# Second attention rebuilt: maxima four pairs ahead, queries turned again by four heads, output rows token-major, last-layer tiles inside

## The reference

```
x = x + attn0(cond(x)); x = x + ffn0(cond2(x))
x = x + attn1(cond3(x)); x = x + ffn1(cond4(x))
```

## Time and profile before

| | |
|---|---|
| median of three runs | 394.83 us (394.56 to 394.91) |
| the profiled execution | 396.64 us, span from first to last instruction 394.9 us |
| mean granted TensorE clock | 0.814 |
| TensorE busy | 265.2 us, 67% |
| VectorE busy | 261.1 us, 66% |
| ScalarE busy | 204.9 us, 52% |
| POOL busy | 43.9 us, 11% |

### The profile page before, as it was taken

One profiled execution on the slowest core, in us unless ns is written; L12 is line 12 of the kernel. 1 busy time (PEld: TensorE's weight loads), 2 busy tenths in 40 slices (PEclk: granted clock), 3 DMA queues, 4 the chain that ended last, 5 costly groups with the idle time before them and its releaser, 6 DMA issues.

```text
span 394.9 us, 5939 instructions
## 1 busy us (share of the span) xinstructions
PE 265.2 (67%) x2278; PEld 166.9 (42%) x2278; DVE 261.1 (66%) x503; ACT 204.9 (52%) x334; POOL 43.9 (11%) x75
## 2 busy tenths in 40 slices
PE   0061778796897866474662875987889798558555
PEld 0050435473473534232241453555656575235413
DVE  2999777989969657989584494263375262893651
ACT  3843686967968675226027247436642663252322
POOL 2201111111111200131220121020000000000000
PEclk9986587998998998776585698597865999967966
DMA  6905525445666650222520039000000000000100
GB/s 132 406 7 109 106 54 108 88 88 100 169 128 127 121 95 0 53 53 56 106 46 7 0 56 264 2 1 2 2 1 0 2 2 0 0 2 13 41 28 27
DMA packets 8812, 25.68 MB, mean 65 GB/s; under 512 B 1616, under 2 KB 3024, under 8 KB 8144
## 3 DMA queue, kind: packets, MB, share of 16 engines
q0 software_dynamic: 4320, 15.73, 21.1%
q1 hardware_dynamic: 4464, 9.57, 7.5%
HBM read 8.52 MB, written 1.05 MB: 24 GB/s over the span
## 4 chain that ended last, share of the span: by engine, by line
PE 42%; DVE 23%; ACT 17%; issue 12%; DMA 4%; POOL 1%; ACTq 0%; DVEq 0%; POOLq 0%
PE PS L1238 6%; PE PM L1186 6%; DVE fwd L660 4%; PE PM L1042 3%; PE PO L1253 3%; PE PM L1126 3%; DVE bwd L668 3%; PE PO L1071 3%; DMA fwd<-bwd 3%; PE PO L1086 3%; PE PM L1112 2%; DVE fwd L930 2%; DVE kp L885 2%; ACT E L568 2%; PE PO L1317 2%
## 5 line engine op out<-in xcount | busy, mean ns | idle before, releaser
L885 DVE TENSOR_REDUCE kp<-PS 128x2 f32<-128x256 f32 x64 | 32.3, 550 | 22.5 <-PE PS L1217 22.4
L568 ACT ACTIVATE E<-PS 128x384 f32<-128x384 f32 x64 | 27.9, 490 | 32.3 <-PE PS L1238 32.3
L495 ACT ACTIVATE E<-PS,negc,escale 128x1024 f32<-128x1024 f32 x32 | 38.2, 1197 | 9.2 <-PE PS L1056 8.6
L1238 PE MATMUL PS<-TP 32*128 32x256 f32 (+1 forms) x128 | 20.6, 428 | 13.6 <-DVE kp L885 7.7
L1086 PE MATMUL PO<-E,vr 128*32 128x256 f32 x256 | 19.2, 421 | 15.1 <-ACT yB L479 11.8
L1186 PE MATMUL PM<-G,sg 128*128 128x512 f32 x32 | 23.1, 886 | 5.0 <-DVE sg L683 5.0
L1016 PE MATMUL PM<-w,sg 128*128 128x256 f32 x32 | 11.1, 510 | 19.7 <-DVE sg L683 19.7
L1238 PEld LDWEIGHTS PS<-TP 32*128 32x128 f32 x128 | 15.5, 235 | 19.6 <-issue 11.2
L1056 PE MATMUL PS<-TP 32*128 32x256 f16 x256 | 20.1, 281 | 3.2 <-DVE TP L710 3.2
L295 POOL DMA_DIRECT2D fwd<-mid x15 | 13.6, 910 | 75.5 <-DVE fwd L660 74.8
L301 POOL DMA_DIRECT2D fwd<-bwd x15 | 13.1, 870 | 77.3 <-DMA fwd<-mid 48.9
(11 more groups left out here) (169 smaller groups left out, 588.0 us busy)
## 6 DMA issues: line engine op xcount, KB each, us to landing
fwd<-mid POOLq DMA_DIRECT2D x15, 512.0 KB, 4.6
fwd<-bwd POOLq DMA_DIRECT2D x15, 512.0 KB, 4.8
G<-in_w SPq DMA_DIRECT2D x2, 1024.0 KB, 10.0
kT<-in_kT SPq DMA_DIRECT2D x4, 256.0 KB, 7.0
xT<-in_xT SPq DMA_DIRECT2D x4, 256.0 KB, 6.4
G<-in_attn SPq DMA_DIRECT2D x1, 1024.0 KB, 6.4
ek<-in_w SPq DMA_DIRECT2D x1, 1024.0 KB, 4.8
ekv<-in_w SPq DMA_DIRECT2D x1, 1024.0 KB, 9.0
```

The source lines that it names most:

```text
L495: nc.scalar.activation(E[:, p % 6], PS[:, 2 * (p % 2):2 * (p % 2) + 2, :], ACT.Exp, bias=negc[:], scale=escale[:]).then_inc(S["e0_done"], 1)
L568: nc.scalar.activation(E[:, p % 4, i, 0:384], PS[:, i, 0:384], ACT.Exp, scale=QSCALE).then_inc(S["e1_done"], 1)
L885: nc.vector.tensor_reduce(kp[:, b % 2, u * H + 2 * j:u * H + 2 * j + 2, D], PS[:, at0:at0 + 2, lo:hi], AX, ALU.max, negate=True).then_inc( ...
L1238: ins = nc.tensor.matmul(PS[:, i, 2 * v * P:2 * P + v * P], k[r:r + ROWS, c, v * P:(v + 1) * P], q[r:r + ROWS, c, v * P:2 * P], start=True ...
```

## The change

- Second attention: LEAD 4 in the place of 11. The lead-in has eight slots and prepares batch 0 only; batch b + 1 is prepared in slots 8b to 8b + 3.
- The queries are turned again by four heads: turn_again(b, c) needs two pairs of maxima, two transposes into bank 1 of PO, and a copy of 128 x 256. Sixteen calls, every second slot.
- rotary reads the swapped halves with one multiplication; for batch 0 VectorE makes the sum too.
- Bank 0 of PO holds values1 and the turned rows of every group (values1(q) waits for the heads of q - 1). Bank 1 is shared in a fixed order, counted by po1_free, by the turned output rows, the re-turned queries, the turned x, the turned hidden values and, for tiles 0 to 3, down.
- The output projection is token-major: project_rows adds x, turned by the identity, and the projected rows in PM bank 1. tanh_rows and x3tok are read from it; the gate of the last conditioning is turned for itself (turn_gates, g3_copy), and gated_rows and quantise work in token order.
- Tables HID_AT, TURN_AT, DOWN_AT, PROJ_AT, ROWS_AT and G3_AT place the last layer. Tiles 0 to 3 run in slots 17 to 30, tiles 4 to 7 in slots 33 to 42. hidden(t) uses the maxima's bank pair (0-1 for tiles 5 and 7).
- Conditionings 13 to 15 are placed anew (LATE), the two scans of a part in two slots.
- The last-layer weights are loaded once, into G[3] and the value tile's space. weight_round moves to slots 20 and 29 of the first attention, weight_ternary to its slots 33 and 35. weight_abs(1) goes before wkv(1), its matmuls from slot 1 to 3, weight_scale from slot 2 to 4.
- In the first attention the residual comes after the first scan part of its slot. The tanh of the third conditioning all come in the feed-forward.

```diff
-        LATE = {BEFORE + 1: (-14, -13, -12, -3, -1), BEFORE + 2: (-10, -9, -7, 5, 7),
-                BEFORE + 3: (-2, 1, 3, 10, 12)}
+        LATE = {BEFORE + 1: (-8, -8, -7, 0, 3), BEFORE + 2: (1, 2, 4, 8, 10),
+                BEFORE + 3: (6, 7, 9, 12, 14)}
...
-        FFN1_SLOT = [B * PAIRS + 2 + t + (6 if t >= TILES - TT else 0) for t in range(TILES)]
-        SLOTS1 = range(-2 * PAIRS, FFN1_SLOT[-1] + 7)
-        LEAD = 11
+        LEAD = 4
+        HID_AT = (17, 19, 25, 27, 33, 34, 38, 39)
+        TURN_AT = (19, 21, 27, 29, 35, 36, 40, 41)
+        DOWN_AT = (20, 22, 28, 30, 36, 37, 41, 42)
+        PROJ_AT = (13, 21, 29, 35)
+        ROWS_AT = (15, 23, 31, 37)
+        G3_AT = (12, 20, 28, 30)
+        SLOTS1 = range(-PAIRS, DOWN_AT[-1] + 1)
...
+        def hid_bank(t):
+            return 0 if t >= TILES - 4 and t % 2 else 2
...
+        PO1, DOWN_USES = {}, {}
+        for p in SLOTS1:
+            for b in turny_at(p):
+                PO1["rows", b] = len(PO1)
+            for key in again_at(p):
+                PO1[("again",) + key] = len(PO1)
+            for t in tiles(TURN_AT, p):
+                PO1["hidden", t] = len(PO1)
+            for t in tiles(DOWN_AT, p):
+                DOWN_USES[t] = len(PO1)
+            for b in tiles(ROWS_AT, p):
+                PO1["x", b] = len(PO1)
...
+                for bb in turny_at(p):
+                    yT1_copy(bb)
+                for bb, c in again_at(p):
+                    again_copy(bb, c)
+                if p % 2 == 0 and 0 <= (p - 2) // 2 < B * CH:
+                    rows_copy((p - 2) // 2, 0, "pv1_done", "turned1_done", "rows1_done")
...
+                for t in tiles(TURN_AT, p):
+                    hqT_copy(t)
+                if j == 1 and b + 1 < B:
+                    v1_copy(b + 1)
+                if j == 2 and b + 1 < B:
+                    qTb_copy(b + 1)
+                if j == 3 and b + 1 < B:
+                    kT1_copy(b + 1)
+                for bb in tiles(G3_AT, p):
+                    g3_copy(bb)
+                for bb in tiles(PROJ_AT, p):
+                    tanh_rows(bb)
+                for t in tiles(HID_AT, p):
+                    square(t)
...
-                rows, hd = 2 * H, D // 2
-                link(nc.vector.tensor_tensor(rot1[u], ps, rope[:, u, 0, None, :].broadcast_to([P, rows, D]), ALU.mult))
-                link(nc.vector.tensor_tensor(rot2[u][:, :, 0:hd], ps[:, :, hd:D],
-                                             rope[:, u, 1, None, 0:hd].broadcast_to([P, rows, hd]), ALU.mult))
-                nc.vector.tensor_tensor(rot2[u][:, :, hd:D], ps[:, :, 0:hd],
-                                        rope[:, u, 1, None, hd:D].broadcast_to([P, rows, hd]),
+                rows = 2 * H
+                first = nc.vector.tensor_tensor(rot1[u], ps, rope[:, u, 0, None, :].broadcast_to([P, rows, D]), ALU.mult)
+                sines = rope[:, u, 1, :].rearrange("p (a e) -> p a e", a=2)
+                nc.vector.tensor_tensor(rot2[u].rearrange("p h (a e) -> p h a e", a=2), swapped,
+                                        sines[:, None].broadcast_to([P, rows, 2, D // 2]),
                                         ALU.mult).then_inc(S["rope_done"], 1)
+                link(first)
...
+            def gated_rows(b):
+                dve.wait_ge(S["tanh_done"], 3 * B + b + 1)
+                dve.wait_ge(S["g3_done"], b + 1)
+                nc.vector.scalar_tensor_tensor(sg[:, seg(b)], sg[:, seg(b)], 1.0, G[3][:, seg(b)], ALU.add,
+                                               ALU.mult).then_inc(S["a_done"], 1)
...
+                elif n >= LEAD:
+                    pe.wait_ge(S["negmax_done"], 2 * n)
                 elif n >= 2:
-                    pe.wait_ge(S["negmax_done"], 2 * (n if n > LEAD else n - 1))
+                    pe.wait_ge(S["negmax_done"], 2 * (n - 1))
+                rounded = [t for t, at in enumerate(HID_AT) if at < n - LEAD]
+                if rounded:
+                    pe.wait_ge(S["relu_done"], len(rounded))
...
+            def free1(key, down):
+                pe.wait_ge(S["po1_free"], PO1[key])
+                if down:
+                    pe.wait_ge(S["res_done"], down)
+
+            def turn_again(b, c):
+                pe.wait_ge(S["negmax_done"], 2 * (PAIRS * b + 2 * c + 2))
+                free1(("again", b, c), downs(PAIRS * b + 2 * c - 2))
+                for u in range(TT):
+                    src = kp[:, b % 2, u * H + 4 * c:u * H + 4 * c + 4, :]
+                    ins = nc.tensor.transpose(PO[:, 1, u * P:(u + 1) * P], src.rearrange("p g s -> p (g s)"), ident[:])
+                ins.then_inc(S["qre_done"], 1)
...
+            def project_rows(b):
+                pe.wait_ge(S["kT1_done"], min(b + 3, B))
+                if b >= 1:
                     pe.wait_ge(S["x3_done"], b)
-                for n, tile in enumerate((sg, xT)):
-                    for u in range(TT):
-                        for k in range(HALF):
-                            at = u * C + k * P
-                            ins = nc.tensor.transpose(PM[:, n, at:at + P], tile[:, seg(b, k * T + u * P, P)], ident[:])
-                ins.then_inc(S["tok_done"], 1)
+                for u in range(TT):
+                    for k in range(HALF):
+                        at = u * C + k * P
+                        nc.tensor.matmul(PM[:, 1, at:at + P], xT[:, seg(b, k * T + u * P, P)], ident[:],
+                                         start=(u == 0 and k == 0), stop=False, skip_group_check=True)
+                pe.wait_ge(S["po1_free"], PO1["rows", b] + 1)
+                for u in range(TT):
+                    for k in range(HALF):
+                        ins = nc.tensor.matmul(PM[:, 1, u * C:(u + 1) * C], yT[:, k, u * P:(u + 1) * P],
+                                               w1a[:, k, 3, :], start=False, stop=(k == HALF - 1), skip_group_check=True)
+                ins.then_inc(S["out1_done"], 1)
...
+                for bb in turny_at(p):
+                    turn_y1(bb)
+                for bb, c in again_at(p):
+                    turn_again(bb, c)
                 if 0 <= p + LEAD < B * PAIRS:
                     maxima(p + LEAD)
-                if p % 2 == 1 and 0 <= (p - 5) // 2 < B * CH:
-                    turn_rows((p - 5) // 2, (p - 5) // 2 % 2, "rows1_done", "turned1_done")
+                if p % 2 == 0 and 0 <= (p - 2) // 2 < B * CH:
+                    values1((p - 2) // 2)
...
+                for bb in tiles(G3_AT, p):
+                    turn_gates(bb)
+                for bb in tiles(PROJ_AT, p):
+                    project_rows(bb)
+                for t in tiles(TURN_AT, p):
+                    turn_hidden(t)
+                for t in tiles(DOWN_AT, p):
+                    down(t)
+                for bb in tiles(ROWS_AT, p):
+                    turn_x(bb)
...
                     hidden(t)
```

More of the change, by code:

```diff
@@ L336, in _ @@
                 link(nc.gpsimd.memset(kp[half[0], :, u * H:(u + 1) * H, at:at + 1], 1.0))
+            pool.wait_ge(S["wq_done"], 2)
+            nc.gpsimd.memset(vt[:, :, :, D:2 * D], 1.0).then_inc(S["v_ones"], 1)
             add_mid(BEFORE)
@@ L806, in _ @@
                         links((p - 3) // 2)
+                    if i == 0 and j == 5 and 1 <= b <= B:
+                        residual("out0_done", b, 0, b - 1)
+                if not parts(p) and j == 5:
+                    residual("out0_done", b, 0, b - 1)
                 if not parts(p) and p % 2 == 1 and 0 <= (p - 3) // 2 < B * CH:
@@ new lines, in _ @@
+                if j == 3 and b + 1 < B:
+                    turn(b + 1, TT * H, "ktr_done", [("qTb_done", b + 2)])
+                for bb in tiles(G3_AT, p):
[4 more added lines that the diff above has]
+                    turn_hidden(t)
+                for t in tiles(DOWN_AT, p):
+                    down(t)
+                for bb in tiles(ROWS_AT, p):
+                    turn_x(bb)
@@ L1352, in _ @@
+                for t in tiles(HID_AT, p):
                     hidden(t)
-                for t in ffn1_tiles(p, 3):
-                    turn_hidden(t)
-                for t in ffn1_tiles(p, 5):
-                    down(t)
 def _channel_major(a):
```

325 lines of the change are left out of this document (162 added, 163 removed).

## The result

| | before | after |
|---|---|---|
| median of three runs | 394.83 us | 379.75 us (379.70 to 383.94) |
| ratio | | 0.966 (0.956 to 0.975) |
| profiled execution, its span | 396.64, 394.9 us | 383.94, 382.1 us |
| mean granted TensorE clock | 0.814 | 0.826 |

The kernel got 15.1 us faster; 28.8 were forecast. The profiled execution of after is the slowest of its three, 4.2 us above the median.

What follows compares the result with a forecast made beforehand. TensorE was taken to bound the slots (92.9 of 110.3 us busy), chains of hand-overs the lead-in and tail. The parts summed 173.0 + 18.9 + 139 + 34.8 = 365.7, forecast 366 us; range 350 to 388, 8 in 10.

Steps and rivals of the forecast that it cites:

- Part A: Up to the second attention's first query/key projection: 173.0 us (165.4 to 178.8) in the place of 169.5.
- Term (1): First attention: absolute sum ahead of wkv(1), its matmuls and weight_scale later; -0.5 us, between -2 and +1.5.
- Term (3): First attention: the two weight roundings on ScalarE move to slots 20 and 29; 2.0 us added, 0 to 4.0.
- Term (4): First attention: the two ternary steps on VectorE move to slots 33 and 35; 2.5 us added, 0 to 3.8.
- Term (2): First attention: the residual add moves behind the first scan part of its slot; -0.5 us, between -2.1 and 0.
- Part B: Second attention's lead-in, up to the first scores: 18.9 us (18 to 24) in the place of 49.1.
- Part C: Second attention's slots 0 to 31: 139 us, TensorE busy 127 and idle 12, in the place of 110.3.
- Rival 1: Second attention's slots: TensorE's clock stays up at 0.92, loop 125 us, total 352; chance 0.17.
- Part D: Tail, from slot 31's exponentials to the end: 34.8 us (31 to 40) in the place of 66.0.
- (2): Rival, second attention's slots: the low clock, 0.69, goes with the dense loop; total 386 us; chance 0.16.
- (3): Rival, second attention's slots: the single bank PO1 bounds, 29 uses add 37 us, total 403; chance 0.11.
- (4): Rival, second attention's slots: tiles 0 to 3 do not get inside; no size or chance given.

Runs made afterwards that it cites:

- scale_back: The changed kernel with the two small matmuls back in slot 1 and weight_scale in slot 2; ratio 0.952, median 376.7 us.
- both_weights: scale_back with the roundings in slots 12 and 28 and the ternaries in 21 and 29; ratio 0.930, median of all six 371.8 us.
- residual_only: The changed kernel with the first attention's residual add back at the head of its slot; ratio 0.961, median 380.4 us.
- turn_x_only: The changed kernel with the turned x and its copy one slot behind the quantising; ratio 0.916, median 363.0 us.
- gaps_filled: both_weights with 14 thrown-away matmuls ahead of TensorE's wait in each of slots 15 and 23; ratio 0.899, compared times 354.3 to 358.5 us.
- both_and_tail: both_weights with tanh_rows ahead of hqT_copy and the last tiles a slot earlier; ratio 0.926, median of all six 369.6 us.
- turn_x_later: both_weights with the turned x and its copy one slot behind the quantising; ratio 0.885, compared times 349.7 to 350.1 us.

## Why the prediction was right in its way and wrong in its size

- **Part A is the step that failed**: 173.0, at most 178.8, against 181.9. Term (1), -0.5: the wait for the absolute sum went, and one for weight_scale came, 4.25 us; the start times have the attention 3.9 us late by slot 20, and scale_back gives 4 us for it at the end. I had named columns0's wait and priced it within 1.5. Term (3), 2.0, at most 4.0: the roundings cost 1.7 and 2.9 us, 4.6 together: the scores of the next exponentials were done at 118.7 and 147.2 us, and the roundings ended at 119.7 and 150.6. Term (4), 2.5: 1.7, so its gaps covered a little more than I gave them. Another 2.2 us, from slot 21 to 29, are in no term. By both_weights the placing of roundings and ternaries is worth 6 to 9 us. Term (2), -0.5: nothing by residual_only, inside its range.
- **Part B**: 18.97 for 18.9. The chain of durations with 0.1 us between held.
- **Part C**: busy 124.4 for 127, the sum by counts and mean durations was good to 2%. Idle 17.3 for 12: of the waits that I named, that in PO1 came as 3.3 us in two, where 1.3 each in three was counted, but turn_x behind its own slot's quantising, 7.3 us, was in no term. It stands in the tables: ROWS_AT gave TensorE and VectorE the same slot, and quantise needs 2.8 us behind whatever VectorE has in it. The sum itself was off too: the waits that it names, 3 x 1.3, 4 x 0.3 and 1.5, are 6.6 and not 8. VectorE and ScalarE were busy for 78.3 and 73.5 us in the loop, not 88 and 86; that neither is the bound held.
- **The clock**: I let the forecast rest on rows in which denser work did not go with a higher clock. Rival 1 put the loop at 125 us if the clock stays up; turn_x_only's is 125.9, at 0.92. What kept the changed kernel from it were the idle stretches of turn_x. The total of 352 was not reached by this edit alone (363), since parts A and D were longer too. That the changed kernel's loop came so near to 139 is partly luck: a wait that I had not priced brought the low clock that I had counted on. The rule that I weighed against those rows (the Trainium skill, "TensorE: Matmul & The Clock Gate", section "HAM oscillation — how this bites in real kernels": gaps throw the array back to its low clock) pointed the right way; gaps_filled, 354 to 358 where both_weights takes 366 to 368, agrees with it. The trace does not bear out more: one wait of 2.31 us went with the low clock in after and not in turn_x_only, and turn_x_only has a low stretch from 226 to 233 us behind waits of 0.74 and 0.61 us alone.
- **Part D**: 39.6 for 34.8. 3.2 us late at the projection, with turn_x ahead of the last values (2.1 of it gone in turn_x_only), and 2 from final(4) ahead of quantise(3), which both_and_tail could not win back: both orders within one slot, which I had walked only for ScalarE.
- **Rivals and signs**: (2) and (3) did not come: PO1 cost TensorE some 6 us of waits in the loop, far from 37. Nor did (4): four tiles ran inside the slots. Of the signs named as wrong one came, a first part that moves by over 5 us: it moved by 12.4.
- The 28.8 us forecast and 15.1 measured differ by 13.7. In the profiled execution the misses add to 16.4 (8.9 A, 0.1 B, 2.7 C, 4.8 D). That execution is 4.2 above the median, and its time is 1.8 above its span, which the forecast left out: 16.4 - 4.2 + 1.8 = 14.0, within 0.3 of the 13.7. Which stage holds the 4.2 us, no other profile of this kernel shows.

## What to carry to other kernels

When work is moved between slots, check for each slot that consumer and producer don't have it in common, engine by engine: turn_x and quantise in one slot cost two waits of 3.6 us and one of 3.1 and, with the clock that followed, 17 us in all. Look for a slot in which the engine waits anyway before a 2 us instruction is put there: the two roundings cost 4.6 us in slots 20 and 29 and nothing that shows in 12 and 28, and that ScalarE is idle for 22% of a stage told neither. A wait of TensorE in this dense loop cost more than its length, 1.3 to 2.2 times by these runs; for another loop that is a first guess, and filling the wait with thrown-away matmuls is the test. Moving the reader by a slot was worth more (17 us) than the fill (12).

## What the hardware showed that was not expected

- Idle stretches of 3.6 us of TensorE were followed by the lower clock, for 7 us in one place and 20 in another: eight score matmuls 1.65 us against 0.92. Two such stretches filled with 14 thrown-away matmuls each left them at 0.92, and the whole kernel 12 us faster.
- The same loop of 927 matmuls was busy for 112.5 us (clock 0.92) or 124.4 (0.82), depending on whether 7.3 us of waits stood in it.
- The same wait of 2.31 us was followed by 10 us at the lower clock in after, and by none in turn_x_only.
- With the fill, the time is still 4 to 9 us above that of turn_x_later: the idle time that it replaces is still spent.
